# Work of the first teams moved into the tail of the attention, and remainders put ahead of marks

## What is computed

```python
def _L1_xattn_ref(query, key_value, ...):
    weights = jax.nn.softmax(scores, axis=-1)          # 16 heads, 112 x 375
    attn = jnp.einsum('bhqk,bhkd->bhqd', weights, V)
    return attn @ Wo.T + bo
def _L1_ffn_ref(hidden_states, wi, bi, wo, bo, lora_A, lora_B, gate_w, gate_b):
    scores = jax.nn.softmax(hidden_states @ gate_w.T + gate_b)
    top_v, top_i = jax.lax.top_k(scores, 2)
    for e in range(E):                                 # E = 8, R = 16
        gate = (top_i == e).sum(-1) * top_v.sum(-1)
        inter = hidden_states @ wi.T + bi + (hidden_states @ lora_A[e].T) @ lora_B[e].T
        out = out + gate[..., None] * (jax.nn.relu(inter) @ wo.T + bo)
x = x + _L1_xattn_ref(_layernorm(x), ctx, ...)
x = x + _L1_ffn_ref(_layernorm(x), ...)
```

## Time and profile before

| | us |
|---|---|
| three runs | 839.5, 830.27, 824.5 |
| their median | 830.27 |
| the profiled execution | 821.05 |
| its span | 819.2 |
| busy in it: TensorE | 725.3 |
| VectorE | 518.1 |
| ScalarE | 331.6 |
| GpSimd | 310.8 |

### The profile page before, as it was taken

One profiled execution on the slowest core, in us unless ns is written; L12 is line 12 of the kernel. 1 busy time (PEld: TensorE's weight loads), 2 busy tenths in 40 slices (PEclk: granted clock), 3 DMA queues, 4 the chain that ended last, 5 costly groups with the idle time before them and its releaser, 6 DMA issues. The chain is left out here.

```text
span 819.2 us, 16531 instructions
## 1 busy us (share of the span) xinstructions
PE 725.3 (89%) x6389; PEld 613.0 (75%) x6389; DVE 518.1 (63%) x1262; ACT 331.6 (40%) x685; POOL 310.8 (38%) x224
## 2 busy tenths in 40 slices
PE   4899999769999999999688989999887868898997
PEld 3678888645588998898566767777665857797997
DVE  4789888858860422213577767877687766656564
ACT  2112221127723221131257767777665442323222
POOL 2233434237830323225235757767585210000000
PEclk9999999969999999999798999999999989999999
DMA  9993001025886654441643876678740000000000
GB/s 292 350 163 47 23 23 45 24 72 171 205 163 117 187 178 136 125 126 14 145 117 66 143 140 124 113 136 226 134 76 2 2 1 12 1 23 1 23 12 24
DMA packets 64475, 81.53 MB, mean 100 GB/s; under 512 B 31892, under 2 KB 54804, under 8 KB 62836
## 3 DMA queue, kind: packets, MB, share of 16 engines
q1 hardware_dynamic: 61170, 72.22, 38.1%
q0 software_dynamic: 2816, 3.67, 2.6%
q10 hardware_dynamic: 416, 4.65, 1.5%
HBM read 60.45 MB, written 19.31 MB: 97 GB/s over the span
## 5 line engine op out<-in xcount | busy, mean ns | idle before, releaser
L1815 DVE TENSOR_REDUCE mx<-psum 112x2 f32<-112x750 f32 x128 | 113.2, 925 | 14.9 <-PE psum L1959 14.5
L1720 ACT ACTIVATE probs<-psum 125x448 f32<-125x448 f32 x192 | 92.4, 544 | 19.6 <-PE psum L1984 17.7
L1641 POOL TENSOR_TENSOR half_sum<-probs 125x896 f32<-125x896 f32 x31 | 66.6, 2149 | 65.7 <-ACT probs L1720 65.7
L556 PE MATMUL psum<-w_parts,c_parts 128*125 128x512 f32 x288 | 74.1, 410 | 11.2 <-DVE w_parts L424 10.8
L1959 PE MATMUL psum<-kpk,qpk 96*112 96x375 bf16 x256 | 62.8, 338 | 14.4 <-DVE mx L1815 11.0
L1984 PEld LDWEIGHTS psum<-qpk,kpk 128*125 128x125 bf16 x768 | 61.8, 140 | 17.2 <-issue 9.1
L556 PEld LDWEIGHTS psum<-w_parts,c_parts 128*125 128x125 f32 x288 | 54.0, 191 | 25.3 <-DVE w_parts L424 10.8
L1984 PE MATMUL psum<-qpk,kpk 128*125 128x112 bf16 x768 | 68.8, 226 | 3.3 <-ACT probs L1720 1.9
L1647 POOL TENSOR_TENSOR tile_sum<-half_sum,probs 125x896 f32<-125x896 f32 x31 | 65.1, 2101 | 2.4
L1148 PE MATMUL psum<-we,hT 128*112 128x256 f32 x256 | 59.9, 395 | 0.0
L2248 PE MATMUL psum<-wo_parts,hs_parts 128*112 128x256 f32 x384 | 51.7, 291 | 9.0 <-DVE hs_parts L2183 8.9
(11 more groups left out here) (231 smaller groups left out, 1502.1 us busy)
## 6 DMA issues: line engine op xcount, KB each, us to landing
we<-in_we SPq DMA_DIRECT2D x6, 2048.0 KB, 8.6
kparts_d<-kp SPq DMA_DIRECT2D x16, 562.5 KB, 5.3
kpk<-kparts_d SPq DMA_DIRECT2D x16, 562.5 KB, 6.2
ctx_all<-in_ctxT SPq DMA_DIRECT2D x16, 375.0 KB, 6.0
kpk<-kparts_d SPq DMA_DIRECT2D x16, 375.0 KB, 7.9
we<-in_we ACTq DMA_DIRECT2D x2, 2048.0 KB, 15.9
kpk<-kparts_d SPq DMA_DIRECT2D x16, 187.5 KB, 8.9
qparts_d<-qp SPq DMA_DIRECT2D x16, 168.0 KB, 3.0
```

The source lines that it names most:

```text
L556: ins = pe.matmul(banks[B_KV[t]][0:KT, :], parts_of[:, x, k, t * KT:(t + 1) * KT], w_parts[:, k, w], start=(k == 0 and (x, w) == SPLIT[0]) ...
L1641: pool.tensor_tensor(half_sum[:, m], probs[:, m, 0], probs[:, m, 1], ALU.add)\
L1720: act.activation(probs[:, m, t, g * HU * SQ:(g + 1) * HU * SQ], banks[B_ST[u % 3]][0:KT, 0:HU * SQ], ACT.Exp, scale=SCALE)\
L1815: dve.tensor_reduce(mx[:, n % 2, H + 2 * j:H + 2 * j + 2], psum[0:SQ, first:first + 2, 0:SK], AX.X, ALU.max)\
```

## The change

- **Where the first team's work stands.** Splits, statistics and normalisation leave j = 4 and 5 and go to `team_ahead(n)`, ahead of the reciprocal (j = 2). The splits of ScalarE's step 13 are taken by VectorE in step 14, those of step 14 in step 15. The order of the ten pieces changes, and seven instead of six are split ahead of the second block (three of them in step 15).
- **The last step's sums.** GpSimd does none of them; `add_up_last` does both halves from `probs`.
- **The tail of the attention.** Statistics of team 1 go into `team_entry`, its power to GpSimd's end, its normalisation behind the last `normalise`. Relu, `second` and `hidden` of units 0 to 3 of the first team are done here, around the last `out_product` and `add_x`.
- **The entry of the second block** is written out for team 0 on each engine: the three splits left (a wi piece, two of wo) stand between units.
- **The other teams.** On VectorE the remainder of unit 6 and `hidden` of unit 7 go ahead of part 3 of `chosen` (the marks). On TensorE `marked` stands behind the first seven units of both products, for all teams.
- The parts of lora_B are in one tile, wi's last quarter is in a tile of the second block.

```diff
-    SPLITS = [("wi", 0), ("lb", 0), ("wi", 1), ("lb", 1), ("wi", 2), ("wi", 3), ("lb", 2), ("lb", 3),
+    SPLITS = [("wi", 0), ("lb", 0), ("wi", 1), ("lb", 1), ("wi", 2), ("lb", 2), ("lb", 3), ("wi", 3),
               ("wo", 0), ("wo", 1)]
+    SPLITS_OF = {B - 3: (0, 1), B - 2: (2, 3), B - 1: (4, 5, 6)}
+    EARLY = 7
...
         for n in range(B):
-            add_tiles(n)
+            if n + 1 < B:
+                add_tiles(n)
             ahead(n)
             if n == TEAM_STATS:
                 inverse_root(pool, 0)
+        inverse_root(pool, 1)
...
+        relu(act, 0, 0)
+        relu(act, 0, 1)
         add_bias(B - 1)
+        relu(act, 0, 2)
+        relu(act, 0, 3)
...
+        def team_ahead(n):
+            if n in (SPLIT_FROM + 1, SPLIT_FROM + 2):
+                for k in SPLITS_OF[n - 1]:
+                    split_low(dve, k)
+            if n == TEAM_STATS:
+                team_statistics(dve, 0)
+            if n == TEAM_NORMAL:
+                ...
+                team_normal(dve, 0)
...
             for j in range(1, H // 2):
+                if j == INVERT_AT:
+                    team_ahead(n)
                 if j == INVERT_AT and n:
                     invert_sums(n - 1)
...
         normalise(B - 1)
+        team_normal(dve, 1)
+        hidden(dve, 0, 0)
+        hidden(dve, 0, 1)
         add_x(B - 1)
+        hidden(dve, 0, 2)
+        hidden(dve, 0, 3)
...
-        for f in range(AHEAD_UNITS):
-            first(pe, 0, f)
+        first(pe, 0, 0)
+        first(pe, 0, 1)
+        first(pe, 0, 2)
+        second(pe, 0, 0)
         out_product(B - 1)
+        first(pe, 0, 3)
+        for f in range(1, AHEAD_UNITS):
+            second(pe, 0, f)
...
+                def entry():
+
+                    first(pe, 0, 4)
+                    team_turn(pe, 1)
+                    first(pe, 0, 5)
+                    second(pe, 0, 4)
+                    gates(pe, 1)
+                    first(pe, 0, 6)
+                    second(pe, 0, 5)
+                    first(pe, 0, 7)
+                    second(pe, 0, 6)
+                    pe.wait_ge(w_low.sem, w_low.at(EARLY + 2))
+                    product(0, 0, range(4))
+                    second(pe, 0, 7)
+                    products_of(0, False, True)
...
-                    for f in range(FC):
-                        hidden(i, f)
+                    for f in range(FC - 1):
+                        hidden(dve, i, f)
...
-                        if more and 3 <= f < 7:
+                        if more and 3 <= f < 6:
                             chosen(dve, f - 3, i + 1)
...
+                    hidden_low(i, FC - 2)
+                    hidden(dve, i, FC - 1)
+                    if more:
+                        chosen(dve, 3, i + 1)
                     hidden_low(i, FC - 1)
```

226 lines of the change are left out of this document (130 added, 96 removed).

## The result

| us, median (lowest to highest) | before | changed | changed / before, 95% interval |
|---|---|---|---|
| first set | 831.13 (824.5–839.5, 4 runs) | 801.85 (796.4–802.6, 4) | 0.968 [0.963, 0.973] |
| second set | 827.32 (814.9–831.8, 11) | 807.59 (804.3–815.3, 6) | 0.986 [0.978, 0.994] |
| third set | 827.64 (820.0–834.2, 11) | 806.77 (805.8–809.6, 6) | 0.977 [0.972, 0.982] |

The changed kernel is faster in all three sets, by the medians 29.3 us in the first and 19.7 and 20.9 us in two later ones; that it is faster by 2% or more only the first interval shows. The intervals take only executions within 1.5% of the fastest of their kernel and the medians take all, which in the second set leaves five of before's eleven, with a median of 820.3 us, and a ratio of 0.986 beside medians that are 2.4% apart.

A forecast was written before the change was run, and what follows sets the result against it. Bound in the changed stages by TensorE's waits on VectorE, partly blocked by GpSimd's sums, and lowered clock. Gains 1.65 + 4.8 + 4.0 + 7.5 = 17.95 us from the 830.27 median give 812.3 us; range 802 to 823, 8 in 10.

The forecast's parts named there:

- Steps 13 and 14: Second attention's steps with early first-team work: 12.7 and 13.9 us expected, gaining 1.65 and 4.8 us.
- 1.5 us of delay: Step 14: allowance for the moved work meeting GpSimd's xb, power and shifted sums ahead of the reciprocal.
- ScalarE's 0.5: Step 14: 0.5 us added for ScalarE itself.
- the collisions move along: Rival: GpSimd blocks the moved work as before, steps 14 and 13 gain only 2 and 1 us; 815.8 us, chance 0.16.
- the extra is not VectorE's: Rival: ScalarE's remaining splits pace steps 13 and 14, so their 6.45 us is not gained; 818.8 us, chance 0.09.
- Reciprocal to block's end: From step 14's reciprocal to the next block's start: 21.17 us grows to 24.0, the barrier 2.8 to 2.9 later.
- The 0.9 us for TensorE's sums: Last attention step: 24 more matmuls, 1.33 us, replace GpSimd's half of the sums, less 0.44 for add_up.
- The entry: Second block's start to the second team's first unit: 30.61 us becomes 23.7, 6.9 gained.
- The 0.7 us for the odds of half clock: Entry: added at even odds that waits halve the clock.
- The teams: Later teams: TensorE's waits of 2.32, 2.32 and 0.92 us and a half-clock stretch go, 7.5 us gained.
- The entry at half clock: Rival: the entry's waits keep the clock low, some 6 us more on the path; 818 us, chance 0.10.
- The slower rival: Chopped entry lowers the clock and the teams behind do not regain it; 848 us if held throughout, chance 0.04.

The follow-up runs named there:

- e5_tail: Changed kernel with relu, second and hidden of units 0 to 3 put back behind the barrier; 805.07 us, 0.981 of before.
- a2_after: The changed kernel itself, unedited, run and traced again in the second set; 807.59 us, 0.986 of before.
- a3_after: The changed kernel itself, unedited, run and traced a third time, in the third set; 806.77 us, 0.977 of before.
- e2_place: Kernel before with only the first team's VectorE splits, statistics and normalisation moved ahead of the reciprocal, splits one step later; 824.28 us, 1.000 of before.
- e6_pool_half: Changed kernel with half 0 of the last step's sums back on GpSimd; 807.86 us, 0.976 of before.
- e4_wo_early: Changed kernel with both VectorE splits of wo put ahead of the entry's sixth hidden; 810.09 us over 4 runs, no interval.
- e4_again: Repeat of the changed kernel with both wo splits ahead of the entry's sixth hidden; 808.34 us, 0.986 of before.
- e1_bodies: Kernel before with only the teams' new order: remainder of unit 6 and eighth hidden ahead of the marks; 814.6 us, 0.990 of before.
- b2_before: The kernel before, unedited, run again for a second trace; 827.42 us, 1.004 of the other runs of before.

## Why the prediction was right, and where not

The forecast was 812.3 us, or 17.95 us less than before. The profiled execution, against which the sum was made, gave 802.6 us where the sum said 803.1: 18.45 us less. The median of the first set, 801.85, lies 0.15 us under the range's lower end; the two later sets, 807.6 and 806.8, lie in it.

- **Steps 13 and 14**, 6.45 us forecast, 7.2 measured (33.04 to 25.85 us), but not as it was laid out. Step 13 was to take 12.7 us and took 14.07, of which 1.67 are the stall that before's trace had not; without it 12.4. e5_tail gives the same figure: 13.18 less a stall of 0.78. Where the clock fell behind a longer stall the subtraction leaves more, 13.9 us in a2_after and 14.7 in a3_after. Step 14 was to take 13.9 and took 11.8 in all three traces. The term "1.5 us of delay" there was mis-sized: the collisions that were feared at that place cost nothing (0.73, 0.41 and 0.72 us) and neither did ScalarE's 0.5. The third pair of splits, for which I had put no collision, did meet GpSimd's sum ahead of step 14's reciprocal and took 1.79 and 0.96 us, within that same 11.8. So the rival that the collisions move along is out, and so is the one that the extra is not VectorE's (e2_place leaves ScalarE's splits in both steps and takes 13.38 and 11.68 us). One row was misread: I took the split of 0.68 us in step 13 for one without a sum of GpSimd beside it. There was one, and it was GpSimd that paid, 3.79 us for 2.08.
- **The statistics** took 1.2 us ahead of the reciprocal. a2_after's step with them took 12.19 us at a clock of 1.00, against 12.16 without: they are free. In the first trace that step took 12.87, at 0.90, behind a stall of 3.50 us in the step ahead of it.
- **Reciprocal to block's end**: 24.0 forecast, 23.64 measured. The 0.9 us for TensorE's sums was 0.77 by e6_pool_half, and the rest fits as a sum.
- **The entry**: 23.7 forecast, 22.69 measured. The waits were 1.21 and 1.14, 2.98, 0.65 and 1.51 us where 1.3, 3.1, 0.9 and 1.4 were put. The 0.7 us for the odds of half clock did not come in this trace; in a3_after's it did, 32.67 us from step 15's end to the second team against 30.2. The longest wait is where it was put, but it is not worth its length: in e4_wo_early and e4_again other waits and the clock take its place.
- **The teams**: 7.5 forecast, 7.7 measured, 7.6 in e1_bodies, which holds that edit alone; the marks are not late, as worked out.
- **Both stretches together**, from step 14's reciprocal to the second team: 4.0 forecast, 5.45 measured (51.78 to 46.33 us). Half clock cost at most 5.2 of the 51.78 (0.17 of 30.61). TensorE's idle time in them fell from 12.8 to 9.6 us (12.4 in b2_before; 8.7 and 9.0 in the later traces of the changed kernel), its busy time from 39.0 to 36.7 with 29 records more. So 3.1 us of the 5.45 are waits and 2.3 are busy time, for which I see no other cause than the clock. e5_tail, with the tail put back, took 50.17 us with 9.5 of it idle: it has the changed kernel's waits and a lower clock.
- **The sum against one trace** is closer (803.1 and 802.6 us) than its terms, and that is luck. Step 14 and the two stretches gained 3.6 us more than forecast; step 13, with its stall, gained 1.4 less, and the 1.9 us lost ahead of step 13 stood in no term.
- **From the sum to the median.** This is the step that holds least. I carried the same 17.95 us over to a median 9 us higher than the profiled execution, without asking where these 9 us stand. Of the 8.8 us between before's two traces 5.0 stand ahead of step 13, which the change does not touch. The mean of the traces falls by 19.0 us from step 13 on and not at all ahead of it, so the 17.95 were 1 us short, and 19.7 and 20.9 us in the later sets agree with that. The 29.3 us of the first set are more than any trace explains: 4 runs on each side, before's median 4 us above that of its later sets and the changed kernel's 5 to 6 below. What was mis-sized is the share of the waits. My sum holds some 10 us of work and waits (17.95 less what half clock cost before, 1.7 in step 14, 1.6 in the second team and 5.2 in the entry, plus the 0.7 put back) and some 8 of clock; measured were 13.8 us of idle time and 5.2 of busy time. Length by one less the clock, summed from step 12 on, is 9.3 and 16.1 us in before's two traces and 1.3, 5.2 and 8.4 in the changed kernel's three; it counts waits at half clock as if they would shorten, and so it gives the clock more than its part.
- **The entry at half clock** came in part: in the two later traces the stretch from step 15's end to the second team ran at 0.94 and 0.90, which cost at most 1.9 and 3.3 us, not 6.
- **The slower rival** needed a clock that stays down behind the entry. In none of the changed kernel's three traces did a wide team run below 1.00. In e4_wo_early, e4_again, e5_tail and e6_pool_half the second team did, at 0.93 to 0.96, and the third was back at 35.5 us in all.

What stays open: why the changed kernel's runs had a mean clock of 0.969 in the first set and 0.960 in the later ones, and why e2_place's gain in the trace is not in its first median. In TensorE's idle time the parts simply add: 6.6 us for the teams' order and 5.8 for the place are 12.4 of the 13.8, and 1.4 are left for the rest of the change, which no run isolates (e5_tail, with the tail put back, has no more idle time than the changed kernel). In the medians they are 12.5 and 2.8 and 5.8 us. That the parts do more together than alone, through the clock, is not shown.

## What to carry to other kernels

Put VectorE's SBUF work where GpSimd rests, and read the gap from GpSimd's timeline rather than from VectorE's: the same 1.9 us of splits and normalisations (unblocked) went with a step of 17.4 us over a busy GpSimd and with one of 11.8 at its rest. Look at both engines for the price, since either may pay it. Price a wait of TensorE by what is late next: a wait of 2.32 us in a full queue of matmuls was worth its whole length, one of 2.98 us in a chain of waits next to nothing. Where the granted clock varies between executions, make the sum from at least two traces of before, see first which part of their difference lies in the stretches that the change touches, and count TensorE's idle time apart from its busy time: here the first repeated within 0.6 us where the whole varied by 6.
